# Own products for the router's logits, token choices in two halves, a new order of the second norm, and 20 filler products for 4

## The reference

```python
x1 = x + L0_conv(norm(x))            # convolutions, linear attention, projection, batch norm
logits = norm(x1) @ gate_w.T         # 8 experts; second layer: 16 experts
top_vals, top_idx = top_k(logits, 2)
w = softmax(top_vals)
x2 = x1 + sum(w_k * expert_k(norm(x1)))      # each token only through its two experts
x3 = x2 + L1_conv(norm(x2))          # softmax attention per image, 256 positions
x4 = x3 + experts(norm(x3))          # 16 gated experts
```

## Time and profile before

| | |
|---|---|
| median of 3 runs (lowest to highest) | 395.77 us (393.26 to 396.43) |
| the profiled execution: its time, its span | 394.16 us, 392.4 us |
| PE busy | 324.9 us, 83% |
| DVE / ACT / POOL busy | 55% / 53% / 49% |
| costliest line | L1373 PE, 96.8 us in 688 passes |
| mean granted clock of PE | 0.914 |

### The profile page before, as it was taken

One profiled execution on the slowest core, in us unless ns is written; L12 is line 12 of the kernel. 1 busy time (PEld: TensorE's weight loads), 2 busy tenths in 40 slices (PEclk: granted clock), 3 DMA queues, 4 the chain that ended last, 5 costly groups with the idle time before them and its releaser, 6 DMA issues. The chain is left out here.

```text
span 392.4 us, 7972 instructions
## 1 busy us (share of the span) xinstructions
PE 324.9 (83%) x2412; PEld 287.9 (73%) x2412; DVE 216.8 (55%) x581; ACT 207.5 (53%) x538; POOL 193.3 (49%) x214
## 2 busy tenths in 40 slices
PE   3999999999796578999999918899546999999900
PEld 1469999999574358999999604689433999999900
DVE  4647755732286816676777354375783344445506
ACT  3552333343365745776766255576464677766314
POOL 6968834330003177757775443100306777777720
PEclk9999999999999569999999967999956899999965
DMA  7344556422391337841111170000031111111147
GB/s 248 147 80 100 122 129 133 87 45 34 70 388 56 109 94 302 297 151 53 55 55 36 52 204 1 1 2 0 0 109 40 56 51 52 55 57 54 49 140 209
DMA packets 34184, 38.47 MB, mean 98 GB/s; under 512 B 3680, under 2 KB 28640, under 8 KB 33376
## 3 DMA queue, kind: packets, MB, share of 16 engines
q1 hardware_dynamic: 22620, 25.79, 22.0%
q0 software_dynamic: 4096, 8.40, 6.8%
q10 hardware_dynamic: 7428, 3.77, 4.2%
HBM read 24.31 MB, written 7.34 MB: 81 GB/s over the span
## 5 line engine op out<-in xcount | busy, mean ns | idle before, releaser
L1373 PE MATMUL bank<-x_cols,w_block 128*128 x688 | 96.8, 286 | 3.6 <-ACT x_cols L693 3.6
L1373 PEld LDWEIGHTS bank<-x_cols,w_block 128*128 128x128 f32 x688 | 88.2, 201 | 5.8 <-issue 5.4
L509 POOL DMA_INDIRECT x_rows<-tok,token x64 | 60.8, 949 | 50.9 <-DVE dest L991 29.5
L516 POOL DMA_INDIRECT y<-wide,dest x64 | 62.1, 970 | 23.0 <-issue 12.8
L1390 PE MATMUL bank<-w_down,h_cols 128*128 x500 | 70.0, 276 | 1.0 <-DVE wide L1056 1.0
L1390 PEld LDWEIGHTS bank<-w_down,h_cols 128*128 128x128 f32 x500 | 62.5, 192 | 1.7 <-issue 1.4
L1283 PEld LDWEIGHTS bank<-cmap,cw 128*128 128x128 f32 x480 | 56.0, 192 | 3.7 <-issue 1.9
L1283 PE MATMUL bank<-cmap,cw 128*128 128x112 f32 (+2 forms) x480 | 57.6, 274 | 0.9 <-DMA cmap<-heads 0.9
L690 ACT ACTIVATE w_block<-w_up 128x512 f32 x86 | 53.4, 621 | 0.9 <-issue 0.7
L319 POOL TENSOR_TENSOR cw<-taps 128x640 f32<-128x640 f32 x24 | 36.9, 1562 | 25.3 <-PE bank L1283 25.3
L1039 DVE TENSOR_TENSOR h_cols<-h_in,bank 128x256 f32<-128x256 f32 x47 | 19.8, 421 | 39.7 <-ACT h_in L707 39.2
(11 more groups left out here) (196 smaller groups left out, 517.6 us busy)
## 6 DMA issues: line engine op xcount, KB each, us to landing
w_up<-in_up_dram SPq DMA_DIRECT2D x4, 1024.0 KB
cmap<-heads SPq DMA_DIRECT2D x48, 64.0 KB
w_up<-in_w_dram SPq DMA_DIRECT2D x1, 2048.0 KB, 7.8
w_down<-in_w_dram SPq DMA_DIRECT2D x1, 2048.0 KB, 13.5
tok<-ln_sq SPq DMA_DIRECT2D x8, 256.0 KB, 2.4
w_down<-in_down_dram SPq DMA_DIRECT2D x4, 512.0 KB
wide<-y SPq DMA_DIRECT2D x8, 256.0 KB, 5.5
ln_sq<-y ACTq DMA_DIRECT2D x8, 256.0 KB, 6.2
```

Of the source, the lines that this page charges most:

```text
L509: pool.indirect_dma_start(out=x_rows[:, j % RING, :], out_offset=None, in_=tok_dram[r], in_offset=bass.IndirectOffsetOnAxis(ap=token[r][:, ...
L516: pool.indirect_dma_start(out=y_dram[r], in_=y_acc[:, s * C:(s + 1) * C], in_offset=None, out_offset=bass.IndirectOffsetOnAxis(ap=dest[r][ ...
L1373: mm = pe.matmul(bank[2 + j % UPS][:, i * 128:(i + 1) * 128], w_block[:, j % 3, i * 128:(i + 1) * 128], x_cols[:, bass.ds(place[j] & ((NB ...
```

## The change

Five things are edited.

1. The logits get products of their own (`token_logits`), with 8 or 16 columns, into banks of their own, and are read there by VectorE; `tok_lg`, its copies and two copies of the centring matrix go. `token_rows` has 128 columns and groups of four tiles; ScalarE's squares wait for TensorE alone.
2. The choices are made in halves of 8 tiles. Tiles 0 to 7 are chosen while the projection's last chunk, or the last images of the attention, are still worked on. `router` does tiles 8 to 15. The inverse norm moves behind the cast of the totals.
3. `token` is computed ahead of the item tables; the waits for `rt_table` are renumbered.
4. In the second norm, ScalarE's roots for chunks 2 and 3 move ahead of the query/key copies of chunks 0 and 1, and VectorE's copies of the values move behind its loop.
5. `keep_clock(4, 4)` becomes `keep_clock(4, 20)`.

```diff
-        ROW_BANKS = ((0, 1, 6, 2, 7, 3), (7, 2, 3, 6, 4, 5))
+        ROW_BANKS = ((6, 7, 2, 3), (3, 6, 4, 5))
+        LOGIT_BANKS = ((0, 1), (7, 2))
...
-                pool.wait_ge(rt_table, 4 * r + 3)
+                pool.wait_ge(rt_table, 4 * r + 1)
...
-                for g, tiles in enumerate(ROW_GROUPS):
-                    act.wait_ge(tok_logits, 6 * r + g + 1)
-                    squares(tiles)
-                    if g == 3:
+                for g in range(4):
+                    act.wait_ge(rows_mm, 4 * r + g + 1)
+                    squares(range(4 * g, 4 * g + 4))
+                    if g == 1:
                         roots(0)
...
             ln_root_of(1)
+            ln_root_of(2)
             query_key_copy(0)
-            ln_root_of(2)
+            ln_root_of(3)
             norm_columns(1)
             query_key_copy(1)
-            ln_root_of(3)
             load_table(ACT.Exp)
...
-                for g, tiles in enumerate(ROW_GROUPS):
-                    a, n = tiles[0], len(tiles)
-                    dve.wait_ge(rows_mm, 6 * r + g + 1)
-                    src = bank[ROW_BANKS[r][g]][:, 0:n * (C + E)].rearrange("p (t q) -> p t q", t=n)
-                    dve.tensor_copy(tok_lg[:, a:a + n, 0:E], src[:, :, C:C + E]).then_inc(tok_logits, 1)
-                dve.wait_ge(tok_logits, 6 * (r + 1))
...
+            def first_choice(r, E, a, b):
+
+                l2, eq, sc, oh1, oh2, m1, d, mx, rk, per_e = choice_views(r, E, a, b)
+                lg = bank[LOGIT_BANKS[r][2 * a // TT]][:, a * E:b * E].rearrange("p (t e) -> p t e", e=E)
+                dve.wait_ge(tok_logits, (b // 8, 2 + b // 2)[r])
+                step(dve.tensor_reduce(m1, lg, AX.X, ALU.max))
+                step(dve.tensor_tensor(eq, lg, per_e(m1), ALU.subtract))
...
+                step(dve.scalar_tensor_tensor(out=sc, in0=eq, scalar=0.0, in1=rk, op0=ALU.is_ge, op1=ALU.mult))
+                step(dve.tensor_reduce(mx, sc, AX.X, ALU.max))
+                step(dve.tensor_tensor(oh1, sc, per_e(mx), ALU.is_equal))
+
+            def second_choice(r, E, a, b):
...
+                step(dve.tensor_tensor(oh2, sc, per_e(mx), ALU.is_equal))
+                dve.tensor_tensor(chosen[:, 0:E, a:b], hots[:, 0, 0:E, a:b], hots[:, 1, 0:E, a:b], ALU.add)\
+                    .then_inc(rt_mask, 1)
+
+            def router(r, E):
+
+                first_choice(r, E, TT // 2, TT)
+                second_choice(r, E, TT // 2, TT)
...
                 step(dve.tensor_tensor(gone, end_at, passed[:, 0:NI, 0:E - 1], ALU.is_lt))
+                dve.wait_ge(rt_inverse, r + 1)
+                step(dve.tensor_copy(place_of[:, :], totals[:, 0:NB]))
+                dve.tensor_scalar(token[r][:, :], place_of[:, :], T - 1, None, ALU.bitwise_and).then_inc(rt_table, 1)
                 step(dve.tensor_reduce(e_f, gone, AX.X, ALU.add))
                 dve.tensor_copy(items[r][:, EXPERT, 0:NI], item[0:1, 0, 0:NI]).then_inc(rt_table, 1)
...
+                    if c == 2:
+                        first_choice(0, E0, 0, TT // 2)
+                    if c == 3:
+                        second_choice(0, E0, 0, TT // 2)
...
-            for c in range(NCH + 2):
+            for c in range(NCH + 1):
...
-                if c >= 3:
-                    value_rows(c - 3)
                 if 1 <= c <= NCH:
                     ln_inverse(c - 1)
+            for c in range(NCH - 1):
+                value_rows(c)
...
+                if i == B - 1:
+                    first_choice(1, E1, 0, TT // 2)
+                if i == B:
+                    second_choice(1, E1, 0, TT // 2)
...
+            def token_logits(r, a, b):
+
+                E = (E0, E1)[r]
+                pe.wait_ge((x1_ready, x3_ready)[r], b // (4, 2)[r])
+                for i in range(a, b):
+                    mm = pe.matmul(bank[LOGIT_BANKS[r][2 * i // TT]][:, i * E:(i + 1) * E], xs[:, i * 128:(i + 1) * 128],
+                                   tok_w[:, r, 0:E], start=True, stop=True)
+                mm.then_inc(tok_logits, 1)
+
...
                 if n == B + 2:
+                    token_logits(0, 0, 8)
                     token_rows(0, 0)
...
-                for g in range(1, 6):
-                    token_rows(r, g)
-                keep_clock(SLOT_BANKS[r][0], 2)
+                if r == 0:
+                    token_rows(0, 1)
+                    token_logits(0, 8, 16)
+                else:
+                    token_logits(1, 14, 16)
+                    token_rows(1, 0)
+                    token_rows(1, 1)
+                token_rows(r, 2)
+                token_rows(r, 3)
+                keep_clock(SLOT_BANKS[r][1], 2)
...
-                pe.wait_ge(rt_table, 4 * r + 2)
+                pe.wait_ge(rt_table, 4 * r + 3)
...
-            keep_clock(4, 4)
+            keep_clock(4, 20)
...
-                if i == B + 2:
-                    token_rows(1, 0)
+                if i >= 4:
+                    token_logits(1, 2 * i - 8, 2 * i - 6)
```

95 lines of the change are left out of this document (39 added, 56 removed).

## The result

The changed kernel took 397.53 us (median of 20 runs, 395.62 to 400.56) against 394.66 us for the kernel before (20 runs on the same chips, 392.31 to 398.66). The ratio is 1.0084, with a 95% interval of 1.0064 to 1.0104: some 3.3 us slower, under one per cent. The forecast was 398.4, +2.6 us. The profiled execution of the changed kernel spans 396.9 us and took 398.77; PE is busy for 343.4 us, 18.5 more than before, of which the 32 more filler passes make most.

A forecast was written before the change was run, and what follows sets the result against it. No engine bounds the whole: TensorE bounds expert stages and attention loop, with hand-over stretches between. Terms +0.15 +4.15 -1.5 -0.3 +0.1 = +2.6 on the 395.77 median give 398.4 us; range 393.2 to 401.2.

The forecast's parts named there:

- Part 2: Router logit products: 0.075 us a narrow pass, upper end 0.119; by the Trainium skill's figure the sum becomes about +3.75.
- Part 1: Second norm: 20 fillers overshoot TensorE's idle hole by 5.0 us and delay the attention by 4.15 us; lower bound -0.35.
- Rival B: Second norm: the hole is usually 17 us long, so fillers don't delay; -0.35 for +4.15, 393.9 us; chance 0.08.
- rival A: Routers: narrow products cost 0.119 a pass; first +1.15 as TensorE's queue clears late, second -0.25; sum +4.85, 400.6 us; chance 0.22.
- Part 3: First router: last residual add 1.38 us later, but VectorE's choice and not TensorE's queue decides the totals; +0.15 us.
- Part 4: Attention's end and second router: early choices help, totals wait for TensorE's rows and fillers instead of the mask; -1.5 us.
- Rival D: Second router: TensorE's queue gates the mask, so early choices don't help; 0 for -1.5, 399.9 us; chance 0.10.
- Part 5: Token indices before item tables: second expert stage -0.3 us (0 to -1.2), first +0.1 (+0.2 to -0.25).
- Rival C: Expert stages: the clock no longer falls in the first items; up to -5 us in both, 393.4 us; chance 0.07.

## Why the prediction was right

The forecast of +2.6 us on the median, 0.7%, met +3.3 (0.84%), from the mechanism that it named, fillers past the end of their hole. Where it was off, terms were mis-sized, and that the sum came this near is in part luck: both routers were set some 0.8 us too good, the fillers 0.3 and the tables 0.5 too bad.

Part 2 rests on one more row of the trace of the kernel before, the one behind the four turns of 39.69:

```profile
40.20 1.04 PE L1283 MATMUL bank<-cmap,cw 128*128 128x128 f32 x8
```

- **Part 1, fillers.** Right, and nearly in size: +4.15 forecast, +3.87 measured at chunk 2's copy, 40 passes in 17.33 us for 17.2, 5.0 us of overshoot, clock 1.00 through the block. The runs with 4 and with 12 fillers show that it is the cause: 4.8 us of the norm stretch come back in each. Rival B's price is confirmed by the run with 12 (393.2 for 393.9), its condition isn't: GpSimd's chunk is ready 11.8 to 12.2 us after the fillers' start in every trace, and 17.3 us don't fit. What I did not work out is what the clock gives back. The overshoot costs 4.8 us in either order. With the old order the clock returns 2.2 of them (4 to 14 fillers), so 20 for 4 cost 2.6 there; with the new order it returns nothing, since root 2 holds the queue at either clock (with 4 and with 12 fillers ScalarE waits 2.33 us for its statistics).
- **Part 2, narrow products.** This step failed. I took 0.075 us from a single narrow pair of products and kept 0.119 as the upper end. It is 0.11 for 8 columns (16 passes in 1.85 us) and for 16 (four passes add 0.45 to a round), the price of a product of 128 columns. The figure in the Trainium skill ("TensorE: Matmul & The Clock Gate", section "LDWEIGHTS (loading the stationary operand)"), the columns over 1.2, so 107 ns for 128, was right against my reading of the row. By rival A's own slope it makes the sum about +4.1 and not the +3.75 that I gave (an estimate: A's shifts of 1.0 and 1.25 us for 0.044 a pass, the first from 0.09 up). My row was two passes read alone. From its start to that of the row above (39.55 to 40.20) lie six passes, the two narrow ones and four turns, so 0.109 each: what the narrow two seemed to save was paid by the passes behind them.
- **Part 3, first router.** The step that follows from it: +0.15 forecast, +0.91 at the totals and +0.83 at the first turn measured; rival A had +1.15. TensorE's queue and VectorE's choice end together there, as A says, but without the fillers the totals come only 0.16 sooner, so A's gate is not the price. It is the last residual add, +2.07 for +1.38, and behind it logits that come late to VectorE.
- **Part 4, second router.** Direction right, -1.5 forecast, -0.67 to -0.95 measured. The terms: +1.34 for +0.9 at the image add, +3.07 for +2.5 at the last one, both from 0.11 a pass. That TensorE's rows and fillers and not the mask hold the totals was right. That the squares lie "just under the inverse" was too: taking the fillers away gains nothing, since they come next. Rival D is refuted: choices put back late cost 0.7 and 1.5 us.
- **Part 5, token indices.** -0.3 forecast with bounds of 0 and -1.2; -0.78 in the traces, 0.69 when undone. The loads of the block table do hold the turn, but the table came 0.5 us later against the totals and not 0.8, and its six loads took 2.3 and not 2.5. First stage: +0.1 forecast, -0.07 measured (11.76 for 11.83), inside the bounds.
- **Rival C, the clock in the first items.** It was given little and did not come. Where it came in another kernel's trace, it brought nothing: in five of those that I use the first group of products took 1.15 us, and the first expert stage 82.8, 83.4, 84.0, 85.2 and 86.4 us; where that group took 2.07 us, the stage took 83.4 to 84.0. In the first three of the five the slow groups merely came one group later. In the last two, 12 fillers and the choices late, the first four groups were fast, and these are the longest stages: the prediction had no term for the gather that TensorE then waits for.

The sum of the parts, with the measured sizes: 0.8 + 3.9 - 0.7 - 0.8 = +3.2. What remains in the span (0.8 ahead of the edits, 0.8 in the first expert stage, -0.3 at the end) lies in the scatter between executions: in these traces that stage takes 82.8 to 86.4 us.

## What to carry to other kernels

Count a filler against the hole it stands in: up to the hole's end it can buy a fast clock, and past it each pass is paid in full (4.8 us here for six products, in either order of the roots). Part of that can be had back where other queues don't hold ready work behind the late result. Fillers and queue orders have to be tried together, since the order that is best at the low clock was the worse one at the high, and with it the fast clock bought nothing. And here a matrix product with 8 or 16 columns cost as much as one with 128, so splitting a narrow result off a wide product doubles the passes for these rows; it pays only where the early result takes more off a chain than the passes add.

## What the runs showed of the hardware that I had not expected

- The clock fell to 0.50 in the midst of unbroken work: 32 passes of 8 columns with their weight loads, PE and PEld both busy 2.00 of 2.00 us, and the clock at 0.85 and then 0.50. With 16 in a row and wide products behind them it stayed at 1.00. It stayed at 0.50 up to 124, through products of 128 and 512 columns, with PE busy all the time.
- A faster start of the expert stage doesn't shorten it, and in the trace with the choices late it was followed by a longer one. TensorE caught up with GpSimd's gathers, which are issued one each 1.25 us, and met one that stood behind the load of an expert's weights and took 6.3 us to its turn. It waited 3.5 us and had the low clock afterwards, when its items come without a pause. The run with 12 fillers shows the same, with a wait of 3.2 us.
- The second expert stage's first turn is set by loads of table values into registers and not by the gather: six loads of 0.33 us fill the 2.36 us from the table to the turn, though the profile names the gather's DMA as the releaser.
